# One attention pass: the last products of a couple issued in two parts, and loops over six couples instead of two

## The reference, cut to what matters

```
q, k, v = fake_quant(x) @ fake_quant(w_qkv).T + b_qkv          # (images, 12, 197, 16)
attn = softmax(fake_quant(q) @ fake_quant(k).T / 4)            # (images, 12, 197, 197)
out  = fake_quant(attn) @ fake_quant(v)
```

## Time and profile before

| | us |
|---|---|
| median of 3 executions (lowest, highest) | 2035.22 (2034.53, 2038.62) |
| profiled execution, its own time | 2038.77 |
| its span, first to last instruction | 2037.0 |
| TensorE busy | 1492.0 (73%) |
| VectorE busy | 1433.1 (70%) |
| ScalarE busy | 1379.6 (68%) |
| GpSimd busy | 1164.9 (57%) |

### The profile page before, as it was taken

One profiled execution on the slowest core, in us unless ns is written; L12 is line 12 of the kernel. 1 busy time (PEld: TensorE's weight loads), 2 busy tenths in 40 slices (PEclk: granted clock), 3 DMA queues, 4 the chain that ended last, 5 costly groups with the idle time before them and its releaser, 6 DMA issues. The chain is left out here.

```text
span 2037.0 us, 50049 instructions
## 1 busy us (share of the span) xinstructions
PE 1492.0 (73%) x12152; PEld 987.7 (48%) x12153; DVE 1433.1 (70%) x3551; ACT 1379.6 (68%) x3956; POOL 1164.9 (57%) x1903
## 2 busy tenths in 40 slices
PE   6999957855656556563688885888864999994563
PEld 6999954411111111111344443554434988884553
DVE  2545559977777777777466666888876777774996
ACT  1323224429999999997799995777662766663885
POOL 2333330046666666663356552577775788884997
PEclk9999978965555555555555555555556999996886
DMA  7654410002222222221554545444434555554785
GB/s 293 256 233 191 163 39 1 1 28 87 83 74 74 76 86 81 76 74 52 124 151 138 151 139 153 137 155 154 151 120 116 134 139 144 145 145 143 224 270 158
DMA packets 184912, 262.77 MB, mean 129 GB/s; under 512 B 28372, under 2 KB 147363, under 8 KB 180328
## 3 DMA queue, kind: packets, MB, share of 16 engines
q1 hardware_dynamic: 137456, 202.16, 32.0%
q0 software_dynamic: 19840, 39.17, 5.4%
q10 hardware_dynamic: 27540, 20.52, 3.1%
HBM read 149.17 MB, written 108.01 MB: 126 GB/s over the span
## 5 line engine op out<-in xcount | busy, mean ns | idle before, releaser
L947 ACT ACTIVATE exps_summed<-s,neg_shift 128x197 f32<-128x197 f32 x1184 | 482.7, 479 | 33.9 <-POOL neg_shift L814 32.7
L984 DVE TENSOR_REDUCE score_max<-s 128x788 f32 (+2 forms) x320 | 284.7, 893 | 107.7 <-PE s L888 95.0
L947 ACT ACTIVATION_READ_ACCUMULATOR exps_summed<-s,neg_shift (+1 forms) x1184 | 304.9, 260 | 0.0
L1346 ACT ACTIVATE exps<-st,scalars 128x788 f32<-128x788 f32 (+1 forms) x320 | 246.4, 889 | 15.4 <-PE st L1255 15.4
L2027 POOL DMA_INDIRECT expert_sums<-y_tile,row_places x216 | 215.5, 998 | 60.3 <-issue 25.6
L367 PE MATMUL mm<-w_tok,x_transposed 128*128 128x192 f32 x1176 | 209.5, 329 | 0.8 <-ACT x_transposed L328 0.8
L888 PE MATMUL s<-k_int,qk_int 16*128 16x197 bf16 x768 | 98.8, 355 | 138.6 <-ACT exps_summed L947 123.4
L328 ACT COPY x_transposed<-tp 128x768 f32<-128x768 f32 x98 | 78.1, 798 | 176.9 <-PE tp L359 176.9
L367 PEld LDWEIGHTS mm<-w_tok,x_transposed 128*128 128x128 f32 x1176 | 190.9, 192 | 1.2 <-ACT x_transposed L328 1.2
L350 POOL TENSOR_SCALAR x_patches<-x_tile 128x768 f32<-128x768 f32 x98 | 81.4, 831 | 188.0 <-PE tp L359 172.2
L1166 POOL TENSOR_SCALAR probs<-exps 128x788 bf16<-128x788 f32 (+1 forms) x160 | 130.0, 819 | 102.5 <-ACT exps L1346 102.4
(11 more groups left out here) (416 smaller groups left out, 4506.1 us busy)
## 6 DMA issues: line engine op xcount, KB each, us to landing
x_tile<-in_x SPq DMA_DIRECT2D x21, 1792.0 KB, 11.0
z_tile<-listed_rows SPq DMA_DIRECT2D x108, 196.0 KB
v_ints<-v_slots SPq DMA_DIRECT2D x32, 480.0 KB
v_slots_in<-v_ints SPq DMA_DIRECT2D x32, 480.0 KB, 3.7
q_ints<-qk_int SPq DMA_DIRECT2D x32, 295.5 KB
k_ints<-k_int SPq DMA_DIRECT2D x32, 295.5 KB
q_shifted<-q_ints SPq DMA_DIRECT2D x32, 295.5 KB, 3.6
k_ones<-k_ints SPq DMA_DIRECT2D x32, 295.5 KB, 4.2
```

The lines of the kernel that those rows point to most:

```text
L947: act.activation(gone[:, v % 2, k], ps[v % 3][:, k, 0:SEQ], ACT.Exp, scale=alpha, bias=nb[:, s, to:to + 1], accum_out=p.lsum[:, bass.ds(n ...
L984: dve.tensor_reduce(columns(m, u), src, op=ALU.max, axis=AXL.X).then_inc(max_done, 1)
L1346: act.activation(ex[:, v % 4, 0:size(u)], src, ACT.Exp, scale=alpha, bias=p.col(C_LNSA)).then_inc(e_ready, 1)
```

## The change

`products_high` takes the list of steps that it issues. Of its five steps (each four matmuls, one for each quarter of the columns, accumulating in the same place) the first two are issued behind unit 8 as before, the other three behind unit 9. Both parts begin with the same wait for `o_out`. In the very last couple, all five are issued together.

The loops go through a new function `couples`: two couples are written out, a loop of four turns takes six couples each, and six couples are written out. With six couples, 60 units, the PSUM area is always the one of the unit three places back: `turn + w` mod 3, where `turn` is n mod 3. The waits are rewritten to the couple's number n. The four `exps` buffers are used in the same order as before. SyncE's loop is not changed.

```
+def couples(eng, body):
+
+    for n in range(2):
+        body(n, n % 2, n // 2, n % 3, False)
+    with eng.Fori(0, (COUPLES - 8) // 6) as i:
+        for k in range(6):
+            body(6 * i + (k + 2), k % 2, 3 * i + (k // 2 + 1), (k + 2) % 3, False)
+    for n in range(COUPLES - 6, COUPLES):
+        body(n, n % 2, n // 2, n % 3, n == COUPLES - 1)
...
                 def _(pe):
-                    def scores(i, s, w):
-                        n, v, u = 2 * i + s, UNITS * s + w, ORDER_OUT[w]
-                        j, x = earlier(i, v, 3)
-                        need(pe, e_ready, ROUND * j + x + 1)
-                        o = ps[v % 3]
+                    def scores(n, s, turn, w):
+                        u = ORDER_OUT[w]
+                        need(pe, e_ready, UNITS * n + (w - 2))
+                        o = ps[(turn + w) % 3]
...
-                    def products_high(n, s):
+                    def products_high(n, s, steps_now):
                         need(pe, o_out, 3 * n)
-                        for t in range(5):
+                        for t in steps_now:
...
-                    def body(i, last):
-                        for s in range(2):
-                            n = 2 * i + s
-                            pe.wait_ge(qk_in[s], 32 * i + 32)
-                            for w in range(UNITS):
-                                scores(i, s, w)
-                                if w == 3 and not (isinstance(n, int) and n == 0):
-                                    ready(1 - s, i - 1 + s)
-                                    products_low(n - 1, 1 - s, 0)
-                                if w == 5 and not (isinstance(n, int) and n == 0):
-                                    products_low(n - 1, 1 - s, 1)
-                                if w == 8 and not (isinstance(n, int) and n == 0):
-                                    products_high(n - 1, 1 - s)
-                    repeat(pe, COUPLES // 2, body)
...
+                    def body(n, s, h, turn, last):
+                        pe.wait_ge(qk_in[s], 32 * h + 32)
+                        for w in range(UNITS):
+                            scores(n, s, turn, w)
+                            if isinstance(n, int) and n == 0:
+                                continue
+                            if w == 3:
+                                ready(n - 1, 1 - s, h - 1 + s)
+                                products_low(n - 1, 1 - s, 0)
+                            if w == 5:
+                                products_low(n - 1, 1 - s, 1)
+                            if w == 8:
+                                products_high(n - 1, 1 - s, (0, 1))
+                            if w == 9:
+                                products_high(n - 1, 1 - s, (2, 3, 4))
+                    couples(pe, body)
...
-                    products_high(COUPLES - 1, 1)
+                    products_high(COUPLES - 1, 1, range(5))
```

More of the change, by code:

```diff
@@ L1151, in attend, with rounded, rounding @@
             ON_POOL = (1, 3, 5, 7, 8)
[L1153 to L1157, removed]
-                else:
-                    need(eng, p_dve, 2 * (UNITS - len(ON_POOL)) * i + v - pool_first + 1)
-            def rounding(eng, sem, tick, i, s, w):
-                n, v, u = 2 * i + s, UNITS * s + w, ORDER_OUT[w]
+            def rounded(eng, n, w):
+                pool_first = sum(x in ON_POOL for x in range(w))
+                if w in ON_POOL:
+                    need(eng, p_pool, len(ON_POOL) * n + pool_first + 1)
+                else:
+                    need(eng, p_dve, (UNITS - len(ON_POOL)) * n + w - pool_first + 1)
+            def rounding(eng, sem, tick, n, s, w):
+                u = ORDER_OUT[w]
                 need_apart(eng, o_done, 12 * (n - 1), tick)
-                need_apart(eng, e_ready, ROUND * i + v + 1, tick)
-                eng.tensor_scalar(pr[:, s, at(u):at(u) + size(u), 0:SEQ], ex[:, v % 4, 0:size(u)], 1.0, 128.0,
+                need_apart(eng, e_ready, UNITS * n + w + 1, tick)
+                eng.tensor_scalar(pr[:, s, at(u):at(u) + size(u), 0:SEQ], ex[:, (2 * s + w) % 4, 0:size(u)], 1.0, 128.0,
                                   ALU.mult, ALU.add).then_inc(sem, 1)
@@ L1229, in _ @@
                     stamps(0, 0, 0)
-                    def body(i, last):
-                        for s in range(2):
-                            n = 2 * i + s
[L1234 to L1239, removed]
+                    def body(n, s, h, turn, last):
+                        for u in range(UNITS):
+                            if u in ON_POOL:
+                                rounding(pool, p_pool, tick_p, n, s, u)
+                            if u == 6 and not last:
+                                stamps(n + 1, 1 - s, h + s)
+                    couples(pool, body)
                     for sem in over:
@@ L1279, in steps, with ready @@
                                 (2 * VP + m * D + SLOT * j, LAST_AT))
[L1281 to L1284, removed]
+                    def ready(n, s, h):
+                        pe.wait_ge(v_in[s], 16 * h + 16)
+                        rounded(pe, n, 8)
+                        rounded(pe, n, 9)
                     def products_low(n, s, m):
@@ L1308, in _, with body @@
                     pe.wait_ge(init_v, 4)
-                    def body(i, last):
-                        for s in range(2):
-                            n = 2 * i + s
-                            pe.wait_ge(qk_in[s], 32 * i + 32)
-                            for w in range(UNITS):
-                                scores(i, s, w)
-                                if w == 3 and not (isinstance(n, int) and n == 0):
-                                    ready(1 - s, i - 1 + s)
-                                    products_low(n - 1, 1 - s, 0)
-                                if w == 5 and not (isinstance(n, int) and n == 0):
-                                    products_low(n - 1, 1 - s, 1)
-                                if w == 8 and not (isinstance(n, int) and n == 0):
-                                    products_high(n - 1, 1 - s)
-                    repeat(pe, COUPLES // 2, body)
-                    ready(1, COUPLES // 2 - 1)
+                    def body(n, s, h, turn, last):
+                        pe.wait_ge(qk_in[s], 32 * h + 32)
[13 more added lines that the diff above has]
+                    couples(pe, body)
+                    ready(COUPLES - 1, 1, COUPLES // 2 - 1)
                     for m in range(2):
                         products_low(COUPLES - 1, 1, m)
-                    products_high(COUPLES - 1, 1)
+                    products_high(COUPLES - 1, 1, range(5))
                     pe.wait_ge(chain, 2)
@@ L1336, in _, with body @@
                     act.reg_load(alpha, p.sc[0:1, C_ALPHA:C_ALPHA + 1].bitcast(I32))
[L1338 to L1348, removed]
+                    def body(n, s, h, turn, last):
+                        for w in range(UNITS):
+                            u = ORDER_OUT[w]
+                            act.wait_ge(s_ready, UNITS * n + w + 1)
+                            if w >= 4:
+                                rounded(act, n, w - 4)
+                            else:
+                                rounded(act, n - 1, w - 4 + UNITS)
+                            src = ps[(turn + w) % 3]
+                            src = src[:].rearrange("p (b k) x -> p b k x", k=2)[:, :, 0, 0:SEQ] if u == 8 else src[:, 0:size(u), 0:SEQ]
+                            act.activation(ex[:, (2 * s + w) % 4, 0:size(u)], src, ACT.Exp, scale=alpha,
+                                           bias=p.col(C_LNSA)).then_inc(e_ready, 1)
+                    couples(act, body)
                 @block.vector
@@ L1376, in peaks, with body @@
                                           axis=AXL.X, apply_absolute_value=True).then_inc(o_abs, 1)
[L1378 to L1388, removed]
+                    def body(n, s, h, turn, last):
+                        for w in range(UNITS):
+                            if w not in ON_POOL:
+                                rounding(dve, p_dve, tick_v, n, s, w)
+                            if w in (5, 7, 9) and not (isinstance(n, int) and n == 0):
+                                outputs(n - 1, (5, 7, 9).index(w))
+                            if w == 1 and not (isinstance(n, int) and n < 2):
+                                peaks(n - 2)
+                    couples(dve, body)
                     for t in range(3):
```

## The result

The changed kernel takes 2034.15 us (median of 20 runs), the kernel before beside it 2037.26 (20 runs): a ratio of 0.9985, 95% interval 0.9978 to 0.9991, so 3.1 us less (1.8 to 4.5). I had forecast 6.8 us less. The time lies on the side forecast and inside my range, but the range says little here: it was set on a median of 3 runs (2035.22), and the median of 20 is 2.0 higher. The gain is what the forecast has to be held to, and it is too small by 3.7 us.

What follows compares the result with a forecast made beforehand. ScalarE was taken to bound the second pass, waiting once per couple for scores 9. 28 x 0.23 = 6.4 us plus 0.39 in the last couple gave 6.8: 2035.22 - 6.8 = 2028.4 us, range 2023.5 to 2036.

Steps and rivals of the forecast that it cites:

- The first part: Two product steps behind unit 8: scores 9 ready at 1.47, before 1.57, removing ScalarE's 0.39 us wait for unit 9.
- The second part: Three product steps behind unit 9 delay scores 0; a new 0.16 us wait at unit 0, net gain 0.23 per couple.
- second wait: TensorE's repeated wait for `o_out` in mid-block, with its register work: taken as nothing, bounds nothing or 0.26 us.
- The bound of 0.26: Upper price of the repeated `o_out` wait, read as delay from an activation's end to weight loads; would cancel the gain.
- Its last term: Time from the start of scores 0 on TensorE to unit 0's activation on ScalarE, taken as 0.57 us.
- register work: Loops on ScalarE, VectorE and GpSimd: changes form, not amount; cost 0, as ScalarE's sequencer works during the 0.80 activation.
- The loads: SyncE's queue: k 0.47 us late for GpSimd in every second couple, but hidden; taken as 0, at most 3.6 us.
- the bound of 5.0: Slowest landing of k in us; it would make k 0.26 us late in some of 14 couples.
- rival (c): The six-couple loop falls out of TensorE's instruction store, fetching at each turn back; 0 to 3.1 us each, 2037.7; chance 0.12.
- The first couples: Start of couples 2 and 3, held by loads of q and k: any gain there is waited away, so none counted.
- the last couple: End of the second pass: gains the whole 0.39 us, as no scores 0 follow.

Runs made afterwards that it cites:

- qk_first: The changed kernel with SyncE issuing q and k of couple n + 1 before v of couple n; ratio to the kernel before 0.9985.
- split_pairs: The kernel before with only the split of the product block, in the old loops over pairs of couples; ratio to the kernel before 0.9978.
- six_whole: The kernel before with only the loops over six couples, all 20 products still behind unit 8; ratio to the kernel before 1.0006.
- after_again: The changed kernel itself, run once more beside the kernel before on another chip; ratio to the kernel before 0.9985.
- act_order: The changed kernel with ScalarE asking first for the rounding of the old exps content, then for the scores; ratio to the kernel before 0.9983.
- whole9: The kernel before with all 20 products behind unit 9 instead of unit 8, loops over pairs; ratio to the kernel before 0.9951.

## Why the forecast was too high

*The first part* held: unit 9 in time, 0.39 gone in each couple.

*The second part* held on TensorE to 0.01 us. Its second wait took nothing, as I had taken it. The bound of 0.26 that I gave for it was misread: that is the idle time of the weight loads, and they start 0.05 after the activation's end (1110.05 + 0.97 against 1111.07). Its last term, 0.57 from scores 0 to the activation, was read at unit 9 of the kernel before and is 0.65 at unit 0 inside a loop. What I wrote on register work, that it changes its form and not its amount and is hidden by 0.80 of activation, was wrong: it is hidden only where ScalarE is not waiting, and unit 0 is now the place where it waits. 0.08 in 22 loop couples is 1.8 us. In three couples (7, 18 and 22) unit 0 was in time and the period 7.52 to 7.56, 0.7 us less in all: there TensorE's clock was granted at its upper level of 2.4 GHz for a part of the time, as the windows of the changed kernel show for one of them (0.67 against 0.50, which is 1.2 GHz; TensorE had been busy for 7.38 of 8 us before).

```profile
1120.00:1128.00 8.00, 7.38 (x126) 3.42 (x122) 5.37 (x13) 7.94 (x11) 4.89 (x9) 0.50 0.49 143
1129.00:1136.00 7.00, 6.04 (x110) 3.14 (x110) 4.71 (x13) 7.00 (x10) 4.19 (x7) 0.67 0.56 164
```

*The loads* are the step that failed, a term that I took at nothing. I had k 0.47 late for GpSimd and bounded the landing by the slowest one in the trace of before, 5.0. In steady couples that was near enough (0.43 below), partly by luck: I had used one landing time, 4.2, for all couples and put the lateness in the even ones. Nine of the 13 waits are in odd couples, whose k is issued 0.5 us sooner but lands more slowly (4.6 for the one issued at 1099.08, 3.3 for the next).

```profile
1103.87 0.54 POOL L1238 TENSOR_TENSOR k_ends<-k_ones,k_rows 128x60 bf16<-128x60 bf16 x2 [0.43 <-DMA k_ones<-k_ints]
```

Two things were missing. The sum asked when GpSimd and the first product block want k, and not when scores 0 do: 5.4 us after its issue at the holes. And the bound of 5.0 did not hold. With nine instruction packets in the stretch the landing took 6.0 to 6.5 at the same two couples in both executions of the changed kernel: in the first, 0.9 and 1.2 us. Another 0.5 is spread over couples 5 (0.16), 8, 19 and 23 (0.37). The last three follow the three short couples, so half of what those gained was given back at once, and not all of it by loads: in qk_first, where nothing waits for k, the couple behind a short one takes 7.83 too. In rival (c) I had asked whether six couples stay in TensorE's store, and they do: no packet comes in the loop's later turns. I had not asked what the loop's first turn and the written-out code fetch (the code holds 14 couples, 6 before), nor whether a fetch delays k. Removing the packets (split_pairs) or giving k room (qk_first) removes the holes, and bringing packets to the unsplit kernel (six_whole) makes one. In the twelve profiles seven loads of k issued after 1010 us took more than 5.3: in the changed kernel, after_again and six_whole those of couples 5 and 27, in act_order that of couple 29. All seven are in kernels with the longer code, and each had such a packet 2.4 to 3.8 us after its issue; none without a packet took over 5.1. That a packet queues ahead of part of k on one engine is my reading of this; it was not followed packet by packet, and other k with a packet at that distance landed in 3.3 to 5.1, so a packet alone does not settle it. That the landing is late, that it is late only with the longer code, and that it costs what it does, is shown.

*The first couples*: "what is gained there is waited away" missed that something is lost there. The load of v of couple 2 waits for the last product, now 0.57 later, and behind it in SyncE's queue stand 24 small transfers and the k of couple 3. Counted from the first activation, this v was issued at 14.3 us before and in six_whole, and at 14.9 in all six profiled executions with the split. From the first activation to couple 3 it was 29.7 us before and in six_whole, 30.2 to 30.4 in five of the six profiled executions with the split, 30.9 in the first one: 0.6 us, and in this profile 1.2. The cause of the other 0.6 was not looked for.

Together, on the 28 periods: 6.4 forecast, less 1.8, 2.1 and 0.5, plus 0.7 of the short couples, is 2.7; 2.8 were measured. With 0.4 for the last couple and 1.2 lost at the start the stage gained 2.0 in this pair of profiles.

The Trainium skill (Runtime: NRT & Kernel Launch, section Instruction fetch mechanics) says that a taken branch to a page outside a window of two pages stalls for the fetch, and gives TensorE's store 2048 instructions. The trace agrees with the second and not with the first: a loop of 1374 matmuls and weight loads, 5.7 packets' worth, went through its three later turns without a packet.

## What to carry to other kernels

When an engine's queue holds work A in front of urgent work B, first ask whether A can move behind B whole: cutting it in two cost two more changes of shape and ended the side-by-side run of scores 9 and 0, and moving the block whole (whole9) gained three times as much: 10 us against 3 in the runs. A wait that has been hidden becomes part of the path once its unit is the late one; in a loop the register operations around it count from then on. Longer loops and more written-out code are fetched by DMA; a load with half a microsecond of room (5.4 against a slowest landing of 5.0) felt it here.

## What was not expected of the hardware

In the changed kernel's trace a 16 KB instruction packet took 0.9 to 1.6 us, and a load of 295 KB in flight with it landed up to 6.5 us after its issue (6.9 in six_whole), against a median of 4.3. The same load landed in 3.2 when the load of v did not stand in front of it. On ScalarE the activation behind a wait that a register operation carried started 0.086 us after that operation (changed kernel, unit 0 at 1105.20); with the wait on the activation itself the couple was that much shorter (act_order).
